# Result matmuls of an attention phase issued per half of the queries, behind successive score tiles

## What is computed

```
h = tok(x)                                   # concat of 3 shifts @ W.T + b
q, k, v = heads(layernorm(h) @ Wq.T / Wk.T / Wv.T)
att = softmax(where(causal, q k^T / sqrt(16), -inf))
h = h + (att v) @ Wp.T + bp
h = h + experts(layernorm(h))                # top 2 of 4, gelu between w1 and w2
```

## Time and profile before

| | us |
|---|---|
| median of 3 runs | 2078.64 |
| lowest and highest run | 2067.15, 2081.69 |
| profiled execution | 2071.52 |
| its span, first to last instruction | 2069.8 |
| TensorE matmuls busy in the span | 1615.3 (78%) |
| VectorE, GpSimd, ScalarE busy | 1052.9, 870.6, 711.7 |

### The profile page before, as it was taken

One profiled execution on the slowest core, in us unless ns is written; L12 is line 12 of the kernel. 1 busy time (PEld: TensorE's weight loads), 2 busy tenths in 40 slices (PEclk: granted clock), 3 DMA queues, 4 the chain that ended last, 5 costly groups with the idle time before them and its releaser, 6 DMA issues. The chain is left out here.

```text
span 2069.8 us, 33551 instructions
## 1 busy us (share of the span) xinstructions
PE 1615.3 (78%) x10648; PEld 1222.6 (59%) x10648; DVE 1052.9 (51%) x3362; ACT 711.7 (34%) x1463; POOL 870.6 (42%) x1024
## 2 busy tenths in 40 slices
PE   3478787787687697787687687515999999999997
PEld 3435364354354364354354343115999999999997
DVE  1255455555455465555555566022555555555554
ACT  0013443343343343433343354301333333333332
POOL 4313333533533633633633623340444544444544
PEclk9758888788789798788788798557999999999999
DMA  2252632732733732732632732219454555555552
GB/s 91 63 91 62 138 80 76 158 80 77 149 85 85 158 84 84 156 87 71 155 86 78 157 81 77 62 48 341 143 185 162 177 180 183 185 189 164 168 180 79
DMA packets 190014, 256.27 MB, mean 124 GB/s; under 512 B 35092, under 2 KB 127182, under 8 KB 189840
## 3 DMA queue, kind: packets, MB, share of 16 engines
q1 hardware_dynamic: 132144, 167.22, 30.6%
q10 hardware_dynamic: 34080, 49.79, 7.9%
q0 software_dynamic: 23616, 37.12, 6.1%
HBM read 173.92 MB, written 75.29 MB: 120 GB/s over the span
## 5 line engine op out<-in xcount | busy, mean ns | idle before, releaser
L582 ACT ACTIVATE prob<-stb 124x496 f32<-124x496 f32 (+2 forms) x832 | 401.4, 504 | 563.4 <-PE stb L937 501.4
L920 PE MATMUL mxb<-kst,qst 96*124 96x372 bf16 (+4 forms) x1024 | 349.2, 373 | 172.0 <-DVE mxp L716 107.1
L713 DVE CUSTOM_DVE_ANT_0 unused<-mxb,mask_row 124x372 bf16<-124x372 f32 (+4 forms) x768 | 352.9, 484 | 147.6 <-PE mxb L920 133.6
L937 PE MATMUL stb<-qst,kst 99*124 99x372 bf16 (+4 forms) x1024 | 331.2, 358 | 61.0 <-DMA qst<-negp 37.9
L1333 PE MATMUL yb<-w2p,hp 128*128 x2448 | 339.9, 283 | 12.7 <-DVE yo L1273 12.7
L920 PEld LDWEIGHTS mxb<-kst,qst 96*124 96x124 bf16 x1024 | 143.9, 152 | 345.6 <-DVE mxp L716 135.3
L1320 PE MATMUL l1b<-x2T,w1s 128*128 128x384 f32 x1632 | 338.4, 343 | 1.2 <-DVE x2T L1232 1.2
L1333 PEld LDWEIGHTS yb<-w2p,hp 128*128 128x128 f32 x2448 | 323.6, 189 | 23.2 <-issue 23.2
L1170 ACT ACTIVATE hf<-l1b,b1c 128x384 f32<-128x384 f32 x272 | 158.0, 581 | 354.5 <-PE l1b L1320 316.9
L1320 PEld LDWEIGHTS l1b<-x2T,w1s 128*128 128x128 f32 x1632 | 276.9, 190 | 1.6 <-DVE x2T L1232 1.6
L960 PE MATMUL pvb<-prob,vaug 124*17 124x372 f32 (+2 forms) x2304 | 228.0, 521 | 41.9 <-POOL prob L516 41.9
(11 more groups left out here) (159 smaller groups left out, 1616.1 us busy)
## 6 DMA issues: line engine op xcount, KB each, us to landing
w1s<-ws SPq DMA_DIRECT2D x34, 2048.0 KB, 8.4
qk_s<-parts SPq DMA_DIRECT2D x192, 93.0 KB
kst<-qk_s SPq DMA_DIRECT2D x192, 93.0 KB, 3.5
xg<-xs SPq DMA_DIRECT2D x34, 396.0 KB
qst<-qk_s SPq DMA_DIRECT2D x32, 279.0 KB, 5.1
wraw<-in_w_all ACTq DMA_DIRECT2D x32, 256.0 KB
ws<-whi ACTq DMA_DIRECT2D x32, 256.0 KB
ws<-wlo ACTq DMA_DIRECT2D x32, 256.0 KB
```

Source lines behind the costliest of these rows:

```text
L582: act.activation(dst, src, ACT.Exp, scale=DH ** -0.5).then_inc(exp_done, 1)
L713: done = dve.tensor_tensor_reduce(out=unused[:, n % 2, e * w:(e + 1) * w], in0=src, in1=mask_row[:, T - w:T], scale=1.0, scalar=-3.0e38, o ...
L920: done = nc.tensor.matmul(out, qst[g % NG][0:ROWS, h + e, TT * i:TT * i + TT], kst[g % NG][0:ROWS, h + e, k0:k0 + w], start=True, stop=True)
L937: done = nc.tensor.matmul(out, kst[g][:, h, TT * j:TT * j + TT], qst[g][:, h, q0:q0 + w], start=True, stop=True)
```

## The change

The result matmuls of a key block are cut into pieces, one for each half of the queries: `PV_PIECES` is the list of (position, half), nine for a group, and `PV_SLOT` the slot of each. The second half of blocks 0, 1 and 2 goes to the slot behind the first (13, 21, 25), and block 5 goes from 28 to 29. The others and the copy keep their slots. `pv_full` is still raised once for a key block, at its last piece. The matmuls themselves, their operands and their order are the same.

```diff
--- before.py
+++ after.py
@@ -58,6 +58,9 @@
 PV_AFTER = (8, 16, 20, 24, 24, 26)
 LEAD = 12
 PV_LAG = 4
+PV_PIECES = [(o, s) for o in range(NT) for s in range(2) if TT * PV_ORDER[o] < (s + 1) * HALF]
+PV_SLOT = (12, 13, 20, 21, 24, 25, 28, 29, 30)
+assert all(t >= PV_AFTER[o] + PV_LAG for t, (o, s) in zip(PV_SLOT, PV_PIECES)) and len(PV_SLOT) == len(PV_PIECES)
 
 
 def later(value):
@@ -96,9 +99,9 @@
 
 def pv_events(g):
 
-    for o in range(NT):
-        yield NST * g + PV_AFTER[o] + PV_LAG, ("pv", (g, o))
-    yield NST * (g + 1) + PV_LAG + 1, ("pv_copy", g)
+    for p, (o, s) in enumerate(PV_PIECES):
+        yield NST * g + PV_SLOT[p], ("pv", (g, o, s))
+    yield NST * g + PV_SLOT[-1] + 1, ("pv_copy", g)
 
 
 def body_events(first, last):
@@ -939,8 +942,9 @@
                             at += w
                         done.then_inc(st_full, 1)
                     if kind == "pv":
-                        g, o = n
+                        g, o, s = n
                         j = PV_ORDER[o]
+                        last = n[1:] == max(p for p in PV_PIECES if p[0] == o)
                         pe.wait_ge(mask_done, b * (NG * NT) + g * NT + o + 1)
                         if o == 0:
                             if g == 0:
@@ -948,19 +952,17 @@
                             if later(b * NG + g):
 
                                 pe.wait_ge(pv_copied, b * NG + g)
-                        for s in range(2):
-                            q0, q1 = max(TT * j, s * HALF), (s + 1) * HALF
-                            if q0 >= q1:
-                                continue
-                            for h in range(HG):
-                                if j in prob:
-                                    p = prob[j][0:TT, h, q0 - TT * j:q1 - TT * j]
-                                else:
-                                    p = prob35[:, h, 0:3 * TT] if j == 3 else prob35[:, h, 3 * TT:4 * TT]
-                                done = nc.tensor.matmul(pvb[2 * DH * h:2 * DH * h + DH + 1, s, q0 - s * HALF:q1 - s * HALF],
-                                                        vaug[:, j, HG * (g % NG) + h, :], p, start=(j == 0),
-                                                        stop=(j == (2 if s == 0 else 4)))
-                        done.then_inc(pv_full, 1)
+                        q0, q1 = max(TT * j, s * HALF), (s + 1) * HALF
+                        for h in range(HG):
+                            if j in prob:
+                                p = prob[j][0:TT, h, q0 - TT * j:q1 - TT * j]
+                            else:
+                                p = prob35[:, h, 0:3 * TT] if j == 3 else prob35[:, h, 3 * TT:4 * TT]
+                            done = nc.tensor.matmul(pvb[2 * DH * h:2 * DH * h + DH + 1, s, q0 - s * HALF:q1 - s * HALF],
+                                                    vaug[:, j, HG * (g % NG) + h, :], p, start=(j == 0),
+                                                    stop=(j == (2 if s == 0 else 4)))
+                        if last:
+                            done.then_inc(pv_full, 1)
 
             over_batches(pe, emit)
 
```

## The result

The changed kernel takes **2085.98 us** (median of 20 runs, 2073.29 to 2095.51), the kernel before 2073.69 (median of 20, 2066.82 to 2085.51). The ratio is 1.0054, interval 1.0037 to 1.0071: slower by 12.3 us by the medians, 11.2 by the ratio (7.7 to 14.7). That is inside the 1% called no change ahead, and inside the range, but it is resolved, and it is about three and a half times the 3.3 us forecast. The time named ahead was 2078, for a kernel before of 2074.8; that part was 1.1 us off.

What follows compares the result with a forecast made beforehand. No engine was full in the attention phase; the bound changes place. Seams +1.2 us per body less credits of 0.9 in seven of eight bodies gave +3.3 us on a mean of 2074.8, so 2078; range 2053 to 2101.

Steps and rivals of the forecast that it cites:

- the 1% called no change ahead: Whole kernel: a difference within 1%, 20.8 us, cannot be told from no change; chance of same 0.62.
- Price of a seam, 0.24 us: TensorE, each added split: 0.10 us on the way in plus 0.14 out; bounds 0 and 0.27.
- The exchange gives nothing back: Score tiles between pieces: earlier feeding is offset by matmul time and seam; value 0, bounds -0.34 and +0.24 us.
- Rival B: Score tiles between pieces arrive while ScalarE and VectorE still have work: 25 us faster, 2050; chance 0.20.
- The other ten lie ahead of one of the waits, cost 0: Slots 24, 38, 46, 50, 54, 64, 72, 76, 80, 98: seams hidden by waits; 2.4 us per body if uncovered.
- Credits of 6.3 us at slots 38 and 46: Earlier q/k products save 0.3 us at slot 38 and 0.6 at 46, in seven bodies.
- Four full places at 0.96 per body: Slots 12, 20, 102 and next body's 2, where TensorE never rests: seams count in full, 4 x 0.24 us.
- Rival A, covers not fixed in time, 31 us: Stalls end later through the mask and exponential chain: all 16 seams count, 30.7 us slower, 2105; chance 0.18.

Runs made afterwards that it cites:

- seam12_20: Kernel before with pieces only at slots 12/13 and 20/21 of head group 0: 2076.90 us, ratio 1.0018 to the kernel before.
- Slot 80: Kernel before with only key block 5 of head group 2 moved from slot 80 to 81: 2083.00 us, ratio 1.0038.
- slot 24: Kernel before with only the second half of key block 2, head group 0, moved from slot 24 to 25: 2079.86 us, ratio 1.0019.
- Slot 72: Kernel before with only the second half of key block 1, head group 2, moved from slot 72 to 73: 2078.38 us, ratio 1.0015.
- Group 1 alone: Kernel before with result matmuls in pieces in head group 1 only (slots 38 to 56): 2075.69 us, ratio 1.0001.
- the group runs: Kernel before with pieces in one head group at a time: groups 0 to 3 took 2083.91, 2075.69, 2082.33 and 2074.05 us.

## Why the prediction was wrong, by its own steps

- **Price of a seam, 0.24 us: right.** 0.22 in the trace after, 0.26 and 0.32 per place in the full stretches, 0.28 at the low clock, and seam12_20 came out as summed (3.7 us, 0.0 to 7.5). The Trainium skill, "TensorE: Matmul & The Clock Gate", "Part 3: Packing small matmuls — row/col tiling", says that a weight load overlaps running matmuls only if its row group differs. By that sentence alone every handover has a seam; the trace after agrees at the borders of the pieces, and again not between max and score tile, where 496 columns need 0.21 us and take 0.22 (928.10 to 928.32). The same section also lets a load into the background weight buffer be pulled ahead, which the prediction left out; by it no seam need stand there.
- **The exchange gives nothing back: right in sign.** ScalarE's waits for score tiles are more and on average shorter (53 in place of 45, 1.21 us in place of 1.37), though the longest is 7.9 us in place of 4.9, and none of the kernels that only cut is faster than before beyond its interval. Rival B is refuted: it priced -25 us.
- **"The other ten lie ahead of one of the waits, cost 0": this step failed.** Slot 80 was in that list and has no wait between it and the next slots' work; behind it the next long wait is that for the mask at slot 90 (1.88 us in the row of 1042.70). The waits nearest to slot 80 stand ahead of it. They are for ScalarE and for a transfer, and they are not among the rows from which the covers were taken, which name 19.1 of the 35.5 us that TensorE was idle in that body:

```profile
PE stb L937 <- ACT prob L582: 5.2, 2, 4.8
...
PE stb L937 <- DMA qst<-negp: 1.7, 1, 1.7
```

  The run at slot 80 stands at the low clock that follows these waits. One place cost 7.9 us (3.7 to 11.8), where even a full seam in each body would have been 2. I had taken a wait somewhere near as cover for each of ten places. Why the price is above the seam stays open. At slot 24, in the same list, more changed than a seam: the second half crossed the wait. Its cost is +3.9 us, -1 to +9, not shown. Slot 72 gave 3.1 (-0.6 to 6.6), not shown either.
- **Credits of 6.3 us at slots 38 and 46: this failed too.** Group 1 alone gave +0.2, and its interval excludes -6.3. At slot 38 GpSimd makes the last part of the product; before:

```profile
964.13 0.89 POOL L533 TENSOR_TENSOR parts<-rest,parts 128x372 bf16<-128x372 f32 x1
```

  After the change (timeline of all engines; SPq is the sync queue):

```profile
973.39 0.48 ACT L637 ACTIVATE parts<-pab 128x372 bf16<-128x372 f32 x1 [1.29 <-PE pab L863]
973.63 0.82 PE L961 MATMUL pvb<-prob,vaug 124*17 124x372 f32 x8
...
975.84 1.43 SPq L420 DMA_DIRECT2D sums<-spare  x1
...
977.31 13.77 SPq L390 DMA_DIRECT2D qk_s<-parts  x9
...
986.68 0.48 ACT L637 ACTIVATE parts<-pab 128x372 bf16<-128x372 f32 x1 [8.37 <-DMA qk_s<-parts]
...
988.24 0.57 PE L923 MATMUL mxb<-kst,qst 96*124 96x372 bf16 x1 [8.68 <-DVE mxp L719]
```

  Counted from the exponential of slot 36 the product is evacuated 2.1 us earlier (1.6 on the mean of six bodies), more than I took. After the change the stores leave at 977.31, when the last fold issue ends (975.84 + 1.43). Before, they left at 965.04, 1.15 us behind the end of the last fold issue and right behind GpSimd's part (964.13 + 0.89): there the product held them. So the queue took a part of what the product had gained, and the stores leave 0.8 us earlier in this body and 0.45 on the mean of six, about the 0.3 credited. But the third product is evacuated no earlier (17.9 us behind slot 36 before, 18.0 after), the stall is 8.68 beside 8.66 in the earlier trace rows, and slots 36 to 46 take 23.1 us before and 23.2 after. Between the first store and the end of the wait the gain is lost; no run shows why. At slot 46 slots 46 to 56 do get 0.3 us shorter (21.4 to 21.0), and group 1 alone shows no gain in time.
- **Four full places at 0.96 per body:** in agreement for 12 and 20; the two of group 3 came out at +1.0 us in all with group 3's others, against 4.8 (-2.9 to 5.0), which is the upper end only.
- **Rival A, covers not fixed in time, 31 us:** its sign was right, its price not. The loss comes from two head groups, not from all sixteen places.

What stays open: how the 11.2 us divide exactly (the group runs sum to 19.7, each uncertain by 4); what makes group 0 cost 10.4 us, as slots 12 and 20 gave 3.7, slot 24 gave 3.9 with an interval that holds zero, and slot 28 was not run alone; and how slot 80 comes to 7.9. In the profiles slots 80 to 84 take 5.88 us with the piece (five kernels) and 5.30 without (thirteen), 0.6 a body and 4.6 us in eight, seam included, but later slots give it back as told above. In the profile of the change itself they take 5.54 beside 5.41 before.

## What to carry to other kernels

A matmul moved by one slot is to be judged place by place; a nearby wait is a cover only if it comes behind the matmul and no other work of the chain stands between, and every wait of the engine has to be on the list, not the longest alone. Cutting a run costs a seam of 0.24 to 0.3 us at every cut and bought nothing here, while moving whole runs into an idle time (and to a slot where their mask was ready) took 2.5% off with the same instructions. And before crediting an earlier product, look at what its store queue is issuing at that moment, and whether the wait at the end of the chain moves too.

## What the hardware showed unexpectedly

- With 124 columns of one run moved a slot on, where TensorE works without a pause at the low clock, the clock stayed at 0.50 to 0.53 through the 6.5 us of slots 80 to 84 in 16 of 30 bodies; without it none of 78 took 6.5 us (the longest 6.4). The columns of work are the same. Yet these bodies were in the end no longer than the others (156.9 us against 157.6 in the four kernels that have both and keep the other runs).
- Bodies of one execution differ: those of the kernel before take 152.9 to 158.0 us with identical instructions, so that a difference of 2.5 us per body is only seen in the mean or in runs.
